# Clearing buffers later and splitting the input statistics in three, in an attention-and-experts kernel

## The reference

```
xn = (x - mean) / sqrt(var + 1e-5)
qkv = xn @ qkv_w.T                       # 32 heads of 8 channels
attn = where(band, q @ k.T * mask * scale, -inf)   # keys i-8 .. i+7
s = softmax(attn) @ v @ proj_w.T + proj_b
e, score = argmax(xn @ router_w), sigmoid(max(xn @ router_w))
h = silu(xs @ gate_w[e]) * (xs @ up_w[e]) ; routed = h @ down_w[e]    # xs = xn * score
shared = silu(xn @ shared_gate_w) * (xn @ shared_up_w) @ shared_down_w
out = x + s * silu(routed + shared)
```

## Time and profile before

| what | us |
|---|---|
| three runs | 613.49, 616.31, 616.04 |
| median | 616.04 |
| profiled execution | 614.93 |
| its span | 613.1 |
| TensorE busy | 550.0 (90%) |
| VectorE busy | 450.6 (73%) |
| ACT busy | 240.7 (39%) |
| GpSimd busy | 232.5 (38%) |

### The profile page before, as it was taken

The page is one execution under the profiler, slowest core; times in us unless marked ns, Lnnn a source line. Parts: engine busy times, 40 slices in busy tenths (PEclk is TensorE's granted clock), DMA queues, the critical chain, the costliest instruction groups (busy, mean ns, idle before and its releaser), DMA issues.

```text
span 613.1 us, 10368 instructions
## 1 busy us (share of the span) xinstructions
PE 550.0 (90%) x3302; PEld 475.3 (78%) x3302; DVE 450.6 (73%) x1045; ACT 240.7 (39%) x506; POOL 232.5 (38%) x172
## 2 busy tenths in 40 slices
PE   1989999979978999999999999999997978789945
PEld 1757899759857999898999898998886757678744
DVE  6777768998767567566567566468999799778984
ACT  1473553437352432523432523444343523243120
POOL 6133323248873232222232232223556653511430
PEclk9989999989999999999999999999998999879987
DMA  9525432113326677676567677543356545421220
GB/s 310 191 76 176 159 130 72 49 47 106 108 96 198 197 190 219 177 216 198 170 183 226 177 199 213 149 128 91 60 121 140 108 111 113 110 58 23 55 57 19
DMA packets 110442, 83.18 MB, mean 136 GB/s; under 512 B 42292, under 2 KB 108724, under 8 KB 110388
## 3 DMA queue, kind: packets, MB, share of 16 engines
q1 hardware_dynamic: 98628, 69.01, 38.2%
q0 software_dynamic: 6144, 8.39, 6.9%
q10 hardware_dynamic: 5616, 5.11, 2.4%
HBM read 59.41 MB, written 23.07 MB: 135 GB/s over the span
## 4 chain that ended last, share of the span: by engine, by line
PE 60%; DVE 17%; issue 6%; DMA 6%; ACT 6%; POOL 4%; SPq 1%; DVEq 0%; ACTq 0%
PE psV L946 12%; PE psM L996 11%; PE psS L921 8%; PE psM L1005 5%; PE psM L973 5%; DMA xnT<-ys_dram,slot 4%; PE psM L896 4%; PE psM L932 3%; DVE O L764 3%; PE psM L901 3%; PE psM L968 3%; DVE PTs L744 3%; PE psM L954 3%; DVE Sx L712 2%; ACT qBD L490 2%
## 5 line engine op out<-in xcount | busy, mean ns | idle before, releaser
L946 PE MATMUL psV<-VB,PTs 128*128 128x132 f32 x1024 | 135.3, 285 | 23.9 <-DVE O L764 23.9
L440 POOL TENSOR_TENSOR Sx<-Sx,mx 128x752 f32<-128x752 f32 x64 | 94.9, 1483 | 154.3 <-DVE mx L722 154.1
L946 PEld LDWEIGHTS psV<-VB,PTs 128*128 128x128 f32 x1024 | 129.6, 196 | 29.3 <-issue 28.2
L434 POOL TENSOR_TENSOR Sx<-Sx,cst 128x752 f32<-128x752 f32 x28 | 46.9, 1677 | 182.5 <-DVE Sx L712 182.5
L921 PE MATMUL psS<-kBD,qBD 128*128 128x188 f32 x512 | 99.3, 326 | 0.2 <-DVE Sx L712 0.2
L921 PEld LDWEIGHTS psS<-kBD,qBD 128*128 128x128 f32 x512 | 85.9, 192 | 9.4 <-issue 2.6
L744 DVE STREAM_TRANSPOSE PTs<-Sx 128x512 f32<-128x512 f32 x128 | 82.8, 685 | 4.2 <-ACT Sx L501 4.2
L712 DVE TENSOR_TENSOR Sx<-psS,cst 128x752 f32<-128x752 f32 x64 | 60.0, 938 | 30.3 <-PE psS L921 29.9
L996 PE MATMUL psM<-xT,EB 128*128 128x128 f32 x624 | 76.5, 276 | 1.6 <-DMA EB<-in_L_ffn_up_w 1.6
L764 DVE TENSOR_TENSOR O<-psV,rs 32x128 f32<-32x128 f32 x256 | 73.5, 287 | 4.8
L996 PEld LDWEIGHTS psM<-xT,EB 128*128 128x128 f32 x624 | 73.8, 192 | 4.0 <-issue 1.9
(11 more groups left out here) (106 smaller groups left out, 671.8 us busy)
## 6 DMA issues: line engine op xcount, KB each, us to landing
EB<-in_L_ffn_gate_w SPq DMA_DIRECT2D x39, 256.0 KB, 3.0
EB<-in_L_ffn_up_w SPq DMA_DIRECT2D x39, 256.0 KB, 3.6
EB<-in_L_ffn_down_w SPq DMA_DIRECT2D x39, 256.0 KB, 3.1
VB<-v_dram SPq DMA_DIRECT2D x256, 32.0 KB
stage<-xs_dram SPq DMA_DIRECT2D x39, 128.0 KB, 2.2
ys_dram<-yb ACTq DMA_DIRECT2D x39, 128.0 KB, 3.2
xs_dram<-blank SPq DMA_DIRECT2D x9, 512.0 KB, 3.1
v_dram<-vS SPq DMA_DIRECT2D x8, 512.0 KB, 3.0
```

Of the source, the lines that this page charges most:

```text
L440: nc.gpsimd.tensor_tensor(s, s, mx[n % 3][:, :].unsqueeze(2).broadcast_to([P, 2 * G, KW]), ALU.subtract).then_inc(a_sub, 1)
L946: last = mm(psV[:, j, at:at + HS * VW], PTs[n % 2][:, k, j, i, :], VB[n % 2][:, i, k, :, VW * j:VW * j + VW], start=k == 0, stop=k == 1)
```

## The change

GpSimd clears only blank, xnT's edges and kBD0 at the start; then it waits until normalise(0) is done, and clears kBD1, VB and Sx and does its casts. s_zero counts 3 in place of 2. The k copies of half batch 0 move from ACT to VectorE (k_out), with a semaphore of their own. The ones in VB are 8 strided memsets in place of 16. LN has three slices, tiles 0 to 3, 4 to 7, and 8 to 31. The first two take the root as before (the code of deviation() now stands in variance()); the third makes 1/sqrt on VectorE alone, by a shift of the bits and three Newton rounds. The order on VectorE is changed: normalise(1) comes ahead of step 0, moments(2) and moments(3) come into step 0 and moments(4) and variance(2) into step 1.

```diff
-LN = ((0, BT), (BT, T))
+LN = ((0, BT), (BT, 2 * BT), (2 * BT, T))
+        mvi = sb("mvi", [P, 2, T], I32)
@@ freed
-                eng.wait_ge(a_qk, 3 * i + ("q", "k0", "k1").index(kind) + 1)
+                if i == 0 and kind != "q":
+                    eng.wait_ge(a_k, int(kind[1]) + 1)
+                else:
+                    eng.wait_ge(a_qk, max(3 * i - 2, 0) + ("q", "k0", "k1").index(kind) + 1)
@@ sync
-            sp.wait_ge(s_zero, 2)
+            sp.wait_ge(s_zero, 3)
@@ gpsimd
-            for i in range(2):
-                zero(kBD[i][:, :, :, :], 0.0)
+            zero(kBD[0][:, :, :, :], 0.0).then_inc(s_zero, 1)
+            pool.wait_ge(n_xn, 2)
+            zero(kBD[1][:, :, :, :], 0.0)
@@ scalar
-                if h == 0:
-                    act.wait_ge(s_zero, 2)
+                if h == 1:
+                    act.wait_ge(s_zero, 3)
-            for kind in ("q", "k0", "k1"):
-                qk_out(kind, 0)
+            qk_out("q", 0)
@@ vector: variance
-                copy(m(7), m(1)).then_inc(s_var, 1)
-
-            def deviation(i):
-                m = lambda k: mv[:, k, slice(*LN[i])]
-                dve.wait_ge(s_sqrt, i + 1)
-                step(nc.vector.reciprocal(m(3), m(2)))
-                step(tt(m(3), m(3), m(1), ALU.mult))
-                step(tt(m(3), m(3), m(2), ALU.add))
-                step(ts(m(3), m(3), 0.5, None, ALU.mult))
-                step(nc.vector.reciprocal(m(6), m(3)))
+                if i < 2:
+                    copy(m(7), m(1)).then_inc(s_var, 1)
+                    dve.wait_ge(s_sqrt, i + 1)
+                    step(nc.vector.reciprocal(m(3), m(2)))
+                    step(tt(m(3), m(3), m(1), ALU.mult))
+                    step(tt(m(3), m(3), m(2), ALU.add))
+                    step(ts(m(3), m(3), 0.5, None, ALU.mult))
+                    step(nc.vector.reciprocal(m(6), m(3)))
+                    return
+                bits = lambda k: mvi[:, k, lo]
+                step(ts(bits(0), m(1).bitcast(I32), 1, None, ALU.arith_shift_right))
+                step(copy(m(3), bits(0)))
+                step(ts(m(3), m(3), -1.0, 1597463007.0, ALU.mult, ALU.add))
+                step(copy(bits(1), m(3)))
+                y = bits(1).bitcast(F32)
+                for k in range(3):
+                    step(tt(m(3), y, y, ALU.mult))
+                    step(tt(m(3), m(3), m(1), ALU.mult))
+                    step(ts(m(3), m(3), -0.5, 1.5, ALU.mult, ALU.add))
+                    step(tt(m(6), y, m(3), ALU.mult))
+                    y = m(6)
+
+            def k_out(j):
+                ps = full(dve, (f"k{j}", 0))
+                dve.wait_ge(s_zero, 2)
+                for i in range(HS):
+                    rows = slice(QB * i, QB * i + QB)
+                    last = copy(kBD[0][rows, j, i, :], ps[rows, 0:KH])
+                last.then_inc(a_k, 1)
@@ vector: weigh
                 if n == 0:
-                    dve.wait_ge(s_zero, 2)
+                    dve.wait_ge(s_zero, 3)
@@ vector: order
             moments(0)
             variance(0)
-            deviation(0)
             normalise(0)
-            for i in range(1, len(GROUPS)):
-                moments(i)
-            dve.wait_ge(s_zero, 2)
+            moments(1)
+            k_out(0)
+            k_out(1)
+            dve.wait_ge(s_zero, 3)
             for v in VB:
                 for h in range(HS):
-                    for c in (0, 2 * VW - 1):
-                        ins = nc.vector.memset(v[QB * h:QB * h + QB, :, :, h, c:c + 1], 1.0)
+                    ins = nc.vector.memset(v[QB * h:QB * h + QB, :, :, h, 0:2 * VW:2 * VW - 1], 1.0)
             ins.then_inc(s_one, 1)
+            variance(1)
+            normalise(1)
             for n in range(LAST + 1):
                 if n < U:
                     weigh(n)
                     if not masked_late(n):
                         largest(n)
                 if n == 0:
-                    variance(1)
-                    deviation(1)
-                if n + 1 < BATCH:
+                    moments(2)
+                    moments(3)
+                if n == 1:
+                    moments(4)
+                    variance(2)
+                if 1 <= n < BATCH - 1:
                     normalise(n + 1)
@@ tensor: scores
                 if u == 0:
-                    pe.wait_ge(a_qk, 3 * h + 3)
+                    pe.wait_ge(a_qk, 3 * h + 1)
+                if n == 0:
+                    pe.wait_ge(a_k, 2)
```

More of the change, by code:

```diff
@@ L246, in build @@
         m_full = [sem(f"m_full{i}") for i in range(MB)]
-        a_qk, a_S, a_mul, a_add, a_max, a_sub, a_exp, a_PT, a_V, a_PV, a_rec, a_nrm, a_OT, a_s = (
-            sem("a_" + n) for n in ("qk", "S", "mul", "add", "max", "sub", "exp", "PT", "V", "PV", "rec", "nrm", "OT", "s"))
+        a_qk, a_k, a_S, a_mul, a_add, a_max, a_sub, a_exp, a_PT, a_V, a_PV, a_rec, a_nrm, a_OT, a_s = (
+            sem("a_" + n) for n in ("qk", "k", "S", "mul", "add", "max", "sub", "exp", "PT", "V", "PV", "rec", "nrm", "OT", "s"))
         x_v, x_vd = ([sem(f"x_{n}{i}") for i in range(2)] for n in ("v", "vd"))
```

## The result

The changed kernel takes 623.41 us in the median of 4 runs (620.80 to 625.14), against 615.71 before: the ratio is 1.0128, 95% interval 1.0083 to 1.0173. It is slower by 7.7 us. I had forecast slower by about 4 and a time of 619.5, and the range ended at 622: direction right, size too small by half. The profiled execution took 622.89, its span 621.1 against 613.1.

What follows compares the result with a forecast made beforehand. It took the chain of waits as the bound, 60% on TensorE and 17% on VectorE, with everything decided in the first 50 us. 614.93 + 3.15 (chain) + 1.5 (clock) = 619.6, forecast 619.5; 8-in-10 range 613.8 to 622.

Steps and rivals of the forecast that it cites:

- Rival (a): The clock stays up at v7 in step 1, for a total of 618.1 us; chance 0.22.
- Rival (c): Statistics of step 1 lie in time TensorE doesn't need, so early gains reach the end: 611.6 to 612.8; chance 0.13.
- Rival (d): The delay is given back later, or low stretches of the second half fall luckier: 614.5 to 616.5; chance 0.13.
- The first root: Ahead of the first normalisation, L629 to L647 run with GpSimd's clears moved away: saves 2.9 to 3.3 us.
- Router wait and k on VectorE: Ahead of weigh(0), v0 waits for router weights; v tiles end at 25.1 instead of 25.9, keeping 0.8 of 3 us.
- rival (b): The clock falls during the router wait, slowing v0 to v3: +1.8 us at weigh(0), total 619.9 to 621.4; chance 0.12.
- The second root: Root behind ACT's v copies, normalise(1) ahead of weigh(0): weigh(0) at 28.1, 0.9 us late.
- Step 0: From weigh(0) to weigh(1), with moments(2) and moments(3) added: weigh(1) at 35.7 instead of 37.86, 2.15 us ahead.
- the +1.7 of my upper bound: In step 0, BN_STATS held by GpSimd's masking would add 1.7 us.
- Step 1: Statistics, Newton steps and normalise(2) ahead of the transposes: L744 starts at 44.5 instead of 41.34, 3.15 us late.
- The clock at v7: After TensorE idles 4.1 us, low clock slows v7 and step 2's scores by 0.9 to 2.2 us, taken as 1.5.

Runs made afterwards that it cites:

- root_early: The changed kernel with the second square root on ACT ahead of the four v copies instead of behind them; 621.86 us, ratio 1.0104.
- warm_half: The changed kernel with 18, 7, 6 and 18 filling matmuls put into four idle times of TensorE; 620.12 us, ratio 1.0066.
- router_early: The changed kernel with the load of the router weights issued right behind the qkv weights; 618.68 us, ratio 1.0066.
- stats_after: The changed kernel with the statistics of step 1 behind VectorE's use of the shared expert's bank; 619.27 us, ratio 1.0054.
- all_three: The changed kernel with router_early, root_early and stats_after together; 614.71 us, ratio 0.9980.
- clears_only: The kernel before with the moved clears and the k copies on VectorE, statistics as before; 617.62 us, ratio 1.0030.
- newton_one: The changed kernel with one Newton round instead of three for tiles 8 to 31; 619.72 us, ratio 1.0051.
- stats_only: The changed kernel with the clears and the k copies put back as before; 622.54 us, ratio 1.0113.

## Why the prediction was wrong in size

The forecast was the right chain with the right sign: a gain at the first root that does not arrive, a new wait behind the v copies, statistics in series in step 1, and a low clock at v7. Rival (a) fell: v7 and the scores of step 2 ran at the low clock. Rival (c) fell: L808 ended at 50.3, not by 44.05. Rival (d) fell: the difference is 8.48 at weigh(2), 8.48 at the routing's first copy (119.04 in the chain, where it was 110.56), and 8.0 at the end. The sum of the forecast up to weigh(2) was 4.65 us, the trace has 8.48. The missing 3.83, step by step:

- **The first root** (saving 2.9 to 3.3): measured 3.35. Right.
- **Router wait and k on VectorE**: the weights landed at 21.9 and not at 21.3, since the loads ahead of them took 0.6 longer to be issued; and the clock fell. I had this as rival (b), a case apart with a chance of 0.12, although the idle time that I gave for it was short: with k ended at 17.5 TensorE idled 4.5 us, not "2 to 3". The eight k matmuls took 2.00 us (the row at 15.50 above), where I had them end at 18.5 by the 2.92 of the row below, so the gap grew. The faster rate shows in these durations only: PEclk reads 1.00 from 10 to 22 us in both kernels. Forecast 25.1 for the end of v3, measured 27.5: 2.4 of the 3.83, 0.6 by the landing and 1.8 by the clock. This is the step that failed: it had the four v tiles at full clock behind a wait of under 3 us. Rival (b) and the forecast's own clock term did not exclude each other, and both came true; even that sum, 621.4, was inside the range. The k copies on VectorE took 0.45 us each, not "at most 0.42", but ended at 20.2, ahead of the weights, and cost nothing here. From the timeline of the kernel before:

```profile
18.97 2.92 PE L901 MATMUL psM<-xnT,wqkv 128*128 128x272 f32 x8
```

- **The second root**: by itself as worked out, 28.04 to 30.48 = 2.44 against the 1.0 and 1.3 worked out, 2.3.
- **Step 0**: 16 tiles in 5.2 us beside GpSimd's masking (the rows at 31.34 and 31.50 above), not held: the +1.7 of my upper bound was not there. The rule of the Trainium skill (SBUF — State Buffer, two separate sides), that a VectorE instruction with one input outside the 2-port modes is not kept out, agrees with these rows. But the copy of the logits, L676, took 1.05 instead of the 0.1 that I wrote for it: GpSimd's subtraction started 0.43 before it, and it was held to its end at 39.02. Before, the subtraction was over when this copy came. I had considered such a hold for the new instructions and not for the old ones that change places. 0.9 of the 3.83. (In root_early this copy took 0.36, and weigh(1) still came 8.49 behind weigh(0), as here, because VectorE had waited 0.60 us for the tanh ahead of L803. So the trace shows the hold, but no run shows how much of the 0.9 would be left without it.)
- **Step 1**: L648 to L670 took 3.45, as forecast to the hundredth. L648 is the first Newton step. The statistics ahead of it were 0.15 shorter than worked out: L630, which stands where L626 stood, took 0.43 instead of 0.6.
- **The clock at v7**: I took 1.5 out of 0.9 to 2.2; it was 2.2 in the profiled execution, 0.7 of the 3.83. The wait ahead of v7 was 3.15 and not the 4.1 that I had, so what I took from the row at 126.86 was the right effect from a longer wait.

Together 2.4 + 0.9 - 0.15 + 0.7 = 3.85. The range ended at 622.0 because I left out what happens when two clock losses and one more held instruction meet; each alone was in reach of the rows.

How much of the 8.48 is each cause, by the runs: the low clock 4.0 (warm_half gives 3.9 back, all of it in two places); the late landing and the root behind it, clock included, 4.6 (router_early); the place of the statistics in step 1, 4.3 (stats_after). These overlap, since the low clock is part of both, and all_three brings back 9.06.

## What to carry to other kernels

When a step comes earlier, list every input of the step behind it with its landing time: here a load of 8 KB, late in the queue and hidden by 0.4 us, ate a gain of 3.3, and the low clock of TensorE behind the idle time cost another 1.8. Work moved into a step costs by what waits behind it on its engine: behind the last use of a shared bank the same statistics were 4.3 us cheaper, clock included. After a reordering, go through the old instructions too for those that now meet a GpSimd instruction, and not only the new ones.

## What the runs showed of the hardware

- TensorE's clock ahead of v0. The idle times were 4.5 (after), 3.9 (clears_only), 4.5 (stats_after), 3.4 (newton_one) and 3.6 us (root_early). After the first four the v tiles ran partly or wholly at 1.2 GHz (5.5, 5.5, 5.5 and 6.8 us for 16 matmuls), after the last they took 3.8. So the length of the gap alone did not decide between 3.4 and 3.9. The Trainium skill (TensorE: Matmul & The Clock Gate, Part 1) says that one kernel has different numbers of cold matmuls from run to run. These rows are one execution each of five kernels: they don't contradict it, and no run here shows it for one kernel.
- Ahead of v7 the idle times were 3.15 (after), 3.19 (stats_only), 4.87 (router_early) and 4.88 us (root_early), and v7 took 2.13, 2.13, 2.13 and 1.66. With 1.63 (newton_one) and 0.87 (warm_half) it took 1.16.
- Eight VectorE copies of 32 x 272 out of PSUM took 3.61 us, 0.45 each with the gap, where ACT's took 0.39 or 0.40.
- The chain of 16 dependent steps on 24 columns took 0.216 us a step, whether it shifts, casts or multiplies; the 8 of newton_one less gave 1.73.
